# Cross attention's row maxima over two banks at once, and a negation moved to GpSimd

## The chip, the cores and the metric

One core of one Trainium2 chip runs the whole program. The metric is the device time of one execution in microseconds, the median of a few runs. Lower is better. The engines in the text are TensorE (PE in the rows), VectorE (DVE), ScalarE (ACT), GpSimd (POOL) and SyncE (SP); PEld is the loading of TensorE's weights. Matmul results go to PSUM, eight banks of 512 fp32 columns on 128 partitions.

## The reference

A decoder block on x of 8 batches, 256 tokens and 128 features: a self-attention with relative position bias, a cross attention to 1601 context tokens, a second self-attention, a dense layer, and a mixture of 8 experts. Cut to the part that the change touches:

```python
x = x + _L0_attn_ref(_layernorm(x), ...)               # first attention, 16 heads of 8, with a position bias
# in _L0_xattn_ref: input_tensor is layernorm(x), ctx_tensor is ctx_1024 (8, 1601, 128)
q = _split_heads(x @ qw + qb)                          # 16 heads of 8
k = _split_heads(ctx @ kw + kb)
v = _split_heads(ctx @ vw + vb)
scores = jnp.einsum('bqhd,bkhd->bhqk', q, k) / np.sqrt(D // H) + mask
probs = jax.nn.softmax(scores, axis=-1)                # over 1601 keys: needs each row's maximum
out = jnp.einsum('bhqk,bkhd->bqhd', probs, v)
```

## The kernel before

The program runs in phases: the first attention ("A"), the cross attention, the second attention ("S"), a dense tail and the experts. The change touches "A" and the cross attention.

**A unit** of the cross attention is one batch and one pair of heads: 8 batches times 8 pairs p are 64 units. Queries and keys are split in bf16 parts and stacked on 54 rows, one head of the pair on partitions 0 to 53 and the other on 64 to 117 (`half`). The scores are made twice. The first time, queries on the partitions, only for the row maxima: 16 products a unit (2 heads, 2 query tiles `qt`, 4 chunks of 401 or 398 keys), which the program calls grains. Each is a matmul at L1220 into one of the four banks of `GRAIN`, read by one `tensor_reduce` of VectorE at L1436 into a column of `MG`. After the 16th, `negate` (L1443) joins the four chunks' maxima and negates them into `MN`; GpSimd splits `MN` in three bf16 parts (`split_maxima`); TensorE turns them (`max_rows`, L1269), ScalarE copies them into rows of the queries (`place_maxima`, L1364), and so the second product, keys on the partitions, comes out with the maximum subtracted. That second product is 13 score tiles a unit (`scores`, `last_tile`, L1238), two matmuls each, into a ring of three banks that other things share; ScalarE takes the exponential of each (L1356). The `values` matmuls (L1258) then sum the exponentials with the values, in three bursts: tiles 0 to 3, 4 to 7, 8 to 12. A copy by ScalarE (L1372) takes the unit's sums and ends it.

**The order** is written by hand. Every engine walks `cross_plan(p)` once a step and runs the entries that are its own; an entry (what, i, ahead) works on the unit `ahead` of the step's. The plan has 13 places j. At place j stands score tile j + 3 (from place 10 on tiles 0, 1, 2 of the next unit, which I write 0', 1', 2'); at places 3, 7 and 12 a burst of values behind it, and at place 7 the transposes of the next unit's maxima ahead of the burst. The grains are of the unit two ahead: 16 spread over the places, at the end of each place's list. At places 5 and 10 of p = 0 to 5 stands a round of preparation of the next batch's context: p 0 and 1 transposes (T), p 2 and 3 key projection (K), p 4 and 5 value projection (V). Units 6 and 7 of a batch have none, nor has the last batch; I call them quiet. At p = 0 stand also the sums of the batch before ("c"), which VectorE divides.

**The waits** around the maxima: grain n waits until VectorE has read grain n - 4 (`m_read`), so that VectorE has up to four banks ahead of it. TensorE runs in order: a grain that waits holds up the score tiles and bursts behind it. A score tile waits until ScalarE has read the ring's bank three turns before.

**The first attention** has 32 units of four heads. VectorE adds the bias and takes the maxima (L988) into `MG`, then negates the unit's 8 numbers (L1001) into `MN`, and GpSimd splits them (from L1028 on).

## Time and profile before

| | us |
|---|---|
| median of 3 runs | 1321.23 |
| lowest and highest run | 1316.71, 1325.92 |
| span of the profiled execution | 1324.9 |
| cross attention's units, first to last join | 256.3 to 880.8 |

The page gives no time of the profiled execution beside its span, which lies inside the runs' range and 3.7 us over their median. All durations in the text are read from that execution. A row of the timeline merges instructions of one kind; its length is from the first one's start to the last one's end, so that x7 in 3.46 us says how closely they follow each other. The bracket at a row's end is the idle time ahead of it and who ended it.

### The profile page before, as it was taken

The page shows a single profiled execution, that of the slowest core. Times are in us where ns is not written, and L with a number is a line of the kernel's source. Part 1 is how long each engine was busy: PE and PEld are TensorE (multiplying, and loading weights), DVE is VectorE, ACT ScalarE, POOL GpSimd, SP SyncE. Part 2 cuts the span into 40 slices and gives each one's busy share as a digit, 9 for nine tenths or more (in the row PEclk, how much of TensorE's full clock was granted, in tenths as well). Part 3 has the DMA queues.
Part 4 walks back from the last instruction along what each step waited for, and adds up shares of the span by engine and source line. Part 5 has one row for each costly group of instructions (what it writes and reads, how often), then busy time and mean ns, then how long its engine had stood idle before and what let it go on. Part 6 is the DMA issues. An engine that isn't in the chain of part 4 may idle for free. (4 is left out here: it accounts for less than half of the span.)

```text
span 1324.9 us, 33276 instructions
## 1 busy us (share of the span) xinstructions
PE 1104.3 (83%) x12028; PEld 602.7 (45%) x12028; DVE 1018.2 (77%) x2779; ACT 869.6 (66%) x1764; POOL 403.8 (30%) x832
## 2 busy tenths in 40 slices
PE   5799995699999999999999999986688878178894
PEld 2344443244444444444444444433344436167773
DVE  7488857588889898898988889956699968755554
ACT  3488873187887878788788787882488744233443
POOL 3211113223050320405023040021624227545552
PEclk9699997699999999999999999997799989588997
DMA  6970005513232132311323113002740022111113
GB/s 164 213 144 30 2 2 138 133 56 84 67 82 68 39 93 84 72 57 34 101 78 81 49 30 85 21 2 58 149 87 2 2 96 72 56 29 39 39 37 111
DMA packets 76648, 92.31 MB, mean 70 GB/s; under 512 B 8463, under 2 KB 62711, under 8 KB 76488
## 3 DMA queue, kind: packets, MB, share of 16 engines
q1 hardware_dynamic: 72392, 83.90, 25.1%
q0 software_dynamic: 2496, 5.12, 1.5%
q8 instruction: 98, 1.61, 0.5%
q10 hardware_dynamic: 1600, 1.18, 0.3%
q14 instruction: 62, 0.51, 0.1%
HBM read 64.37 MB, written 27.02 MB: 69 GB/s over the span
## 5 line engine op out<-in xcount | busy, mean ns | idle before, releaser
L1436 DVE TENSOR_REDUCE MG<-bank 128x1 f32<-128x401 f32 (+1 forms) x1024 | 515.4, 566 | 75.3 <-PE bank L1220 73.6
L1356 ACT ACTIVATE PT<-bank 128x512 f32<-128x512 f32 (+1 forms) x624 | 334.6, 597 | 64.3 <-PE bank L1238 63.8
L1238 PE MATMUL bank<-QP,KP 54*128 54x256 bf16 (+1 forms) x1664 | 252.4, 274 | 16.3 <-DVE CAT L1451 4.1
L1220 PE MATMUL bank<-KP,QP 54*128 54x401 bf16 (+1 forms) x1024 | 237.0, 344 | 14.8 <-DMA KP<-ctx_k_parts 9.6
L1258 PE MATMUL bank<-PT,VP 128*9 128x256 f32 (+1 forms) x2688 | 197.3, 367 | 0.8 <-ACT XT L1356 0.8
L1511 POOL TENSOR_TENSOR MP<-MN,ZERO 128x4 bf16<-128x4 f32 x128 | 26.4, 206 | 440.8 <-DVE MN L1443 435.8
L1238 PEld LDWEIGHTS bank<-QP,KP 54*128 54x128 bf16 (+1 forms) x1664 | 110.4, 96 | 108.3 <-ACT PT L1356 24.4
L1220 PEld LDWEIGHTS bank<-KP,QP 54*128 54x128 bf16 x1024 | 75.5, 94 | 125.0 <-DVE MG L1436 94.4
L1356 ACT ACTIVATE XT<-bank 128x512 f32<-128x512 f32 (+1 forms) x208 | 116.2, 599 | 20.3 <-PE bank L1238 19.9
L896 PE MATMUL bank<-QP,KP 51*128 51x256 bf16 x512 | 95.7, 281 | 33.6 <-ACT QP L827 8.8
L1258 PEld LDWEIGHTS bank<-PT,VP 128*9 128x9 f32 (+1 forms) x2688 | 76.0, 90 | 57.6 <-issue 20.4
L863 PE MATMUL bank<-KP,QP 51*128 51x256 bf16 x512 | 97.8, 287 | 4.3 <-DVE MN L994 1.4
L988 DVE CUSTOM_DVE_ANT_0 JUNK<-bank,UQ 128x256 bf16<-128x256 f32 x256 | 92.1, 420 | 6.8 <-PE bank L863 6.6
L951 ACT ACTIVATE XT<-bank 128x512 f32<-128x512 f32 x128 | 74.1, 604 | 32.6 <-PE bank L896 32.0
L1258 PE MATMUL bank<-XT,VP 128*9 128x256 f32 (+1 forms) x896 | 91.2, 367 | 0.0
L994 DVE TENSOR_REDUCE MN<-bank 128x2 f32<-128x512 f32 x128 | 81.8, 685 | 4.2 <-POOL MP L1045 1.2
L1028 POOL TENSOR_TENSOR MP<-MN,ZERO 128x8 bf16<-128x8 f32 x128 | 26.4, 206 | 187.8 <-DVE MN L1001 112.4
L896 PEld LDWEIGHTS bank<-QP,KP 51*128 51x128 bf16 x512 | 33.2, 95 | 103.4 <-issue 43.4
L2041 PE MATMUL bank<-WUP,XP 128*128 x234 | 67.8, 427 | 14.6 <-DVE XP L2210 13.5
L827 ACT COPY QP<-bank 3x512 bf16<-3x512 bf16 x96 | 54.8, 571 | 32.4 <-PE bank L932 32.0
L1364 ACT COPY QP<-bank 3x256 bf16<-3x256 bf16 x128 | 45.3, 354 | 26.5 <-DMA q_parts<-PT 25.7
L2218 DVE TENSOR_TENSOR AC<-SI,bank 128x512 f32<-128x512 f32 x39 | 26.8, 688 | 45.5 <-issue 20.7
(281 smaller groups left out, 2007.5 us busy)
## 6 DMA issues: line engine op xcount, KB each, us to landing
KP<-ctx_k_parts SPq DMA_DIRECT2D x128, 100.1 KB
ctx_k_parts<-KPARTS SPq DMA_DIRECT2D x16, 600.4 KB
KP<-ctx_k_parts SPq DMA_DIRECT2D x128, 59.4 KB
CN<-in_ctx SPq DMA_DIRECT2D x8, 768.0 KB
RAW<-in_w_gate_up SPq DMA_DIRECT2D x8, 512.0 KB, 3.8
QP<-q_parts SPq DMA_DIRECT2D x20, 192.0 KB
ctx_k_parts<-KPARTS SPq DMA_DIRECT2D x16, 200.1 KB
UQ<-bias_table SPq DMA_DIRECT2D x4, 768.0 KB, 8.5
```

The costliest lines, as they stand in the source:

```text
L827: last = copy(k.QP[rows, p:p + 2, b * S:(b + 1) * S], PM[:, :].bitcast(BF16)[rows, 0:2 * S].rearrange("r (j n) -> r j n", j=2))
L863: last = nc.tensor.matmul(bank[:, S * qt:S * (qt + 1)], k.QP[rows, p, a:a + 128], k.KP[rows, p, b * S:(b + 1) * S], start=True, stop=True)
L896: last = nc.tensor.matmul(bank[:, S * t:S * (t + 1)], k.KP[half(s), p, a:a + 128], k.QP[half(s), p, b * S:(b + 1) * S], start=not bias, st ...
L951: nc.scalar.activation(PT[n % 8], SCORE[n % 3][:, :], ACT.Exp).then_inc(exp_done, 1)
L988: last = nc.vector.tensor_tensor_reduce(out=JUNK[:, 2 * (n % 2) + q, :], in0=bank[:, S * q:S * (q + 1)], in1=k.UQ[:, 2 * p + s, 128 * q:12 ...
L994: nc.vector.tensor_reduce(MN[:, u % 3, j, s, :], bank[:, :].rearrange("p (q n) -> p q n", q=QT), AX.X, ALU.max, negate=True).then_inc(grai ...
L1220: nc.tensor.matmul(GRAIN[n % NG][:, 0:w], k.QP[half, p, b * S + 128 * qt:b * S + 128 * (qt + 1)], k.KP[half, p, a:a + w], start=True, stop ...
L1238: return nc.tensor.matmul(bank[0:rows[t], S * at:S * (at + 1)], k.KP[half, p, 128 * t:128 * t + rows[t]], k.QP[half, p, b * S:(b + 1) * S] ...
L1258: last = nc.tensor.matmul(k.PO[32 * c:32 * c + HD + 1, q:q + w], VP[b % 2][0:rows[t], t, 2 * p + s, :], PT[(T * g + n) % NP][0:rows[t], S ...
L1356: nc.scalar.activation(PT[n % NP][0:rows[t], :], bank_of("s", g, t)[0:rows[t], :], ACT.Exp).then_inc(exp_done, 1)
L1436: nc.vector.tensor_reduce(MG[:, g % 4, 2 * s + qt, chunk:chunk + 1], GRAIN[n % NG][:, 0:w], AX.X, ALU.max).then_inc(m_read, 1)
L2041: last = nc.tensor.matmul(bank[j % 2], XP[:, j % 2, a, :], WUP[:, bass.ds(e, 1), b, n0:n0 + FF].rearrange("p a n -> p (a n)"), start=(n == ...
```

## The change

In the cross attention the four grain banks become one tensor of four banks, of which `DOUBLE` is banks 0 and 1, or 2 and 3. A grain is now a double: the products of both heads for one query tile and one chunk, into two neighbouring banks, and one `tensor_reduce` of VectorE reads both (128 x 2 x 401) and writes two maxima. A unit has 8 of them. A double waits until the double two before it has been read. `cross_plan` puts the doubles at places 0, 2, 3, 5, 6, 8, 10 and 11, and the join and the split, which stood at the end of a step, behind the first double of the next step (its `ahead` goes from 2 to 1 with that, so it is the same unit's). In the first attention the negation leaves VectorE: GpSimd takes 0 minus the maxima ahead of its split, and waits for that.

```diff
-    k.BANK = [k.stack.enter_context(nc.psum_tensor(f"bank{i}", [128, 512], F32)) for i in range(8)]
+    k.FOUR = k.stack.enter_context(nc.psum_tensor("bank", [128, 4, 512], F32))
+    more = [k.stack.enter_context(nc.psum_tensor(f"bank{i}", [128, 512], F32)) for i in range(4, 8)]
+    k.BANK = [k.FOUR[:, i, :] for i in range(4)] + [bank[:, :] for bank in more]
...
-            def negate(u, i):
-                v.wait_ge(grain_read, 4 * u + 4)
-                if u >= 3:
-                    v.wait_ge(max_split, 4 * (u - 2))
-                nc.vector.tensor_scalar(MN[:, u % 3, :, :, :], MG[:, u % 3, :, :, :], -1.0, None,
-                                        ALU.mult).then_inc(neg_ready, 1)
...
             def split_maxima(u, i):
-                if bias:
-                    pl.wait_ge(neg_ready, u + 1)
-                else:
-                    pl.wait_ge(grain_read, 4 * u + 4)
+                pl.wait_ge(grain_read, 4 * u + 4)
                 if u >= 3:
                     pl.wait_ge(m_turned, u - 2)
+                if bias:
+                    flat = MG[:, u % 3, :, :, :].rearrange("p j s q -> p (j s q)")
+                    nc.gpsimd.tensor_tensor(MN[:, u % 3, :, :, :].rearrange("p j s q -> p (j s q)"),
+                                            ZERO[:, :].broadcast_to(list(flat.shape)), flat,
+                                            ALU.subtract).then_inc(neg_ready, 1)
+                    pl.wait_ge(neg_ready, u + 1)
...
+    doubles = {0: 0, 2: 1, 3: 2, 5: 3, 6: 4, 8: 5, 10: 6, 11: 7}
...
-        plan += [("g", g, 2) for g in range(G * (j + 1) // T if j else 0, min(G, G * (j + 2) // T))]
-    return plan + [("o", 0, 0), ("neg", 0, 2), ("split", 0, 2)]
+        if j in doubles:
+            plan.append(("g", doubles[j], 2))
+        if j == 0:
+            plan += [("neg", 0, 1), ("split", 0, 1)]
+    return plan + [("o", 0, 0)]
...
-                if n >= NG:
-                    pe.wait_ge(m_read, n - NG + 1)
+                if n >= 2:
+                    pe.wait_ge(m_read, n - 1)
...
-                nc.tensor.matmul(GRAIN[n % NG][:, 0:w], k.QP[half, p, b * S + 128 * qt:b * S + 128 * (qt + 1)],
-                                 k.KP[half, p, a:a + w], start=True, stop=True).then_inc(m_ready, 1)
+                for s in (first, 1 - first):
+                    half = slice(HALF * s, HALF * s + CROSS_ROWS)
+                    last = nc.tensor.matmul(DOUBLE[n % 2][:, s, 0:w],
+                                            k.QP[half, p, b * S + 128 * qt:b * S + 128 * (qt + 1)],
+                                            k.KP[half, p, a:a + w], start=True, stop=True)
+                last.then_inc(m_ready, 1)
...
-                nc.vector.tensor_reduce(MG[:, g % 4, 2 * s + qt, chunk:chunk + 1], GRAIN[n % NG][:, 0:w],
+                nc.vector.tensor_reduce(MG[:, g % 4, :, qt, chunk], DOUBLE[n % 2][:, :, 0:w],
                                         AX.X, ALU.max).then_inc(m_read, 1)
```

How the order moves is shown for three places of a quiet unit. The first is TensorE's, from the first burst of values to the transposes of the maxima. Here L1220 are grains, L1238 (L1240 in the changed kernel) score tiles and L1269 (L1271) the transposes; the burst stands right ahead of the first row. Before:

```order
3083 L1220 MATMUL bank<-KP,QP 128x401 x2
3084 L1238 MATMUL bank<-QP,KP 128x256 x2
3085 L1220 MATMUL bank<-KP,QP 128x398
3086 L1238 MATMUL bank<-QP,KP 128x256 x2
3087 L1220 MATMUL bank<-KP,QP 128x398
3088 L1238 MATMUL bank<-QP,KP 128x256 x2
3089 L1220 MATMUL bank<-KP,QP 128x401
3090 L1238 MATMUL bank<-QP,KP 128x256 x2
3091 L1269 MATMUL bank<-IDB,MP 3x128 x4
```

and in the changed kernel the same stretch of TensorE:

```order
2671 L1220 MATMUL bank<-KP,QP 128x401 x2
2672 L1240 MATMUL bank<-QP,KP 128x256 x4
2673 L1220 MATMUL bank<-KP,QP 128x398 x2
2674 L1240 MATMUL bank<-QP,KP 128x256 x2
2675 L1220 MATMUL bank<-KP,QP 128x401 x2
2676 L1240 MATMUL bank<-QP,KP 128x256 x2
2677 L1271 MATMUL bank<-IDB,MP 3x128 x4
```

The three single grains have become two doubles, the second of them (the unit's fifth, d4) ahead of the last score tile.

The second place is TensorE's, from the end of the second burst to the third burst, which follows the last row. Before:

```order
3096 L1220 MATMUL bank<-KP,QP 128x401 x2
3097 L1238 MATMUL bank<-QP,KP 128x256 x2
3098 L1238 MATMUL bank<-QP,KP 65x256
3099 L1220 MATMUL bank<-KP,QP 128x401
3100 L1238 MATMUL bank<-QP,KP 65x256
3101 L1220 MATMUL bank<-KP,QP 128x398
3102 L1238 MATMUL bank<-QP,KP 128x256 x2
3103 L1220 MATMUL bank<-KP,QP 128x401
3104 L1238 MATMUL bank<-QP,KP 128x256 x2
3105 L1220 MATMUL bank<-KP,QP 128x401
3106 L1220 MATMUL bank<-KP,QP 128x398
3107 L1238 MATMUL bank<-QP,KP 128x256 x2
```

and in the changed kernel, same engine, same stretch:

```order
2682 L1240 MATMUL bank<-QP,KP 128x256 x2
2683 L1240 MATMUL bank<-QP,KP 65x256
2684 L1220 MATMUL bank<-KP,QP 128x401 x2
2685 L1240 MATMUL bank<-QP,KP 65x256
2686 L1240 MATMUL bank<-QP,KP 128x256 x2
2687 L1220 MATMUL bank<-KP,QP 128x401 x2
2688 L1240 MATMUL bank<-QP,KP 128x256 x2
2689 L1220 MATMUL bank<-KP,QP 128x398 x2
2690 L1240 MATMUL bank<-QP,KP 128x256 x2
```

Two grains stood between the burst and score tile 11; now tile 11 comes first and the double d5 behind it. Two grains or one double (d7) stand ahead of the last row, tile 2'.

The third place is VectorE's, the first two units of the cross attention (L1436 and L1438 are the reduces, L1443 and L1445 the join). Before:

```order
767 L1436 TENSOR_REDUCE MG<-bank 128x1 x16
768 L1443 TENSOR_REDUCE MN<-MG 128x4
769 L1436 TENSOR_REDUCE MG<-bank 128x1 x16
770 L1443 TENSOR_REDUCE MN<-MG 128x4
```

and in the changed kernel:

```order
735 L1438 TENSOR_REDUCE MG<-bank 128x2 x9
736 L1445 TENSOR_REDUCE MN<-MG 128x4
737 L1438 TENSOR_REDUCE MG<-bank 128x2 x8
738 L1445 TENSOR_REDUCE MN<-MG 128x4
```

The join of a unit has moved behind the next unit's first reduce, and half as many reduces stand between two joins.

## Rows read from the trace of the kernel before

**Rows 1.** The page: the span, and busy time of each engine.

```profile
span 1324.9 us, 33276 instructions
...
PE 1104.3 (83%) x12028; PEld 602.7 (45%) x12028; DVE 1018.2 (77%) x2779; ACT 869.6 (66%) x1764; POOL 403.8 (30%) x832
```

**Rows 2.** Eight cross units by windows: stretch, its length, busy us (instructions), clock, DMA.

```profile
410.00:490.00 80.00, 75.15 (x897) 36.18 (x895) 70.27 (x152) 64.88 (x137) 20.60 (x48) 1.00 0.24 65
```

**Rows 3.** The page, costliest groups: two reduces of VectorE that read PSUM.

```profile
L1436 DVE TENSOR_REDUCE MG<-bank 128x1 f32<-128x401 f32 (+1 forms) x1024 | 515.4, 566 | 75.3 <-PE bank L1220 73.6
...
L994 DVE TENSOR_REDUCE MN<-bank 128x2 f32<-128x512 f32 x128 | 81.8, 685 | 4.2 <-POOL MP L1045 1.2
```

**Rows 4.** Line L1443, the join of a unit's maxima: ns min/median/max, first and last start.

```profile
L1443 DVE TENSOR_REDUCE MN<-MG x64: 169/170/171, 256.3 to 880.8; 128x4 f32<-128x16 f32 x64
```

**Rows 5.** Timeline, ScalarE: the copies that end units 60, 61 and 62.

```profile
871.79 0.37 ACT L1372 COPY OT<-bank 128x256 f32<-128x256 f32 x1 [0.52 <-PE bank L1258]
...
880.58 0.37 ACT L1372 COPY OT<-bank 128x256 f32<-128x256 f32 x1 [0.51 <-PE bank L1258]
...
888.77 0.37 ACT L1372 COPY OT<-bank 128x256 f32<-128x256 f32 x1 [0.27 <-PE bank L1258]
```

**Rows 6.** Timeline, TensorE, one quiet unit: start, length, line, tile, count.

```profile
646.18 0.28 PE L1238 MATMUL bank<-QP,KP 54*128 54x256 bf16 x1
...
648.56 0.34 PE L1220 MATMUL bank<-KP,QP 54*128 54x401 bf16 x2
...
650.38 0.23 PE L1269 MATMUL bank<-IDB,MP 128*3 128x128 bf16 x2 [0.19 <-ACT XT L1356]
...
651.46 0.34 PE L1220 MATMUL bank<-KP,QP 54*128 54x401 bf16 x2
...
651.64 0.38 PE L1238 MATMUL bank<-QP,KP 54*128 54x256 bf16 x3
...
652.95 0.82 PE L1220 MATMUL bank<-KP,QP 54*128 54x401 bf16 x2
...
653.44 0.39 PE L1238 MATMUL bank<-QP,KP 54*128 54x256 bf16 x2
...
654.96 0.28 PE L1238 MATMUL bank<-QP,KP 54*128 54x256 bf16 x1
```

**Rows 7.** Timeline, VectorE, the same unit.

```profile
648.93 2.50 DVE L1436 TENSOR_REDUCE MG<-bank 128x1 f32<-128x401 f32 x5 [0.21 <-PE bank L1220]
...
651.84 3.46 DVE L1436 TENSOR_REDUCE MG<-bank 128x1 f32<-128x401 f32 x7 [0.41 <-PE bank L1220]
...
655.33 0.17 DVE L1443 TENSOR_REDUCE MN<-MG 128x4 f32<-128x16 f32 x1
```

**Rows 8.** Timeline, ScalarE, the same unit.

```profile
652.06 2.52 ACT L1356 ACTIVATE PT<-bank 128x512 f32<-128x512 f32 x5 [0.26 <-PE bank L1238]
```

**Rows 9.** Timeline, all engines, a unit with two rounds of key projection.

```profile
605.53 0.37 ACT L1372 COPY OT<-bank 128x256 f32<-128x256 f32 x1 [0.63 <-PE bank L1258]
...
611.24 0.34 PE L1220 MATMUL bank<-KP,QP 54*128 54x401 bf16 x2
...
611.83 0.60 ACT L1356 ACTIVATE PT<-bank 128x512 f32<-128x512 f32 x1 [0.23 <-PE bank L1238]
...
612.48 0.94 PE L1291 MATMUL bank<-CT,WQK 128*128 128x401 f32 x2
...
615.52 0.37 ACT L1372 COPY OT<-bank 128x256 f32<-128x256 f32 x1 [0.49 <-PE bank L1258]
```

**Rows 10.** Timeline of the first attention: VectorE's idle time, GpSimd's last split, TensorE's next transposes.

```profile
143.35 0.06 DVE L986 MEMSET TOUCH<- 1x1 f32 x1 [0.91 <-PE bank L863]
...
143.38 0.21 POOL L1045 TENSOR_TENSOR MP<-MN,MP 128x8 bf16<-128x8 f32 x1
...
145.08 0.33 PE L932 MATMUL bank<-IDB,MP 128*3 128x128 bf16 x5
```

**Rows 11.** Timeline, VectorE, the first cross unit's maxima.

```profile
248.44 7.79 DVE L1436 TENSOR_REDUCE MG<-bank 128x1 f32<-128x401 f32 x16 [9.28 <-PE bank L1220]
```

More of the change, by code:

```diff
@@ L136, in allocate @@
     k.HALF = k.sb("HALF", [128, NT])
-    k.BANK = [k.stack.enter_context(nc.psum_tensor(f"bank{i}", [128, 512], F32)) for i in range(8)]
-    k.RING = [bank[:, :] for bank in k.BANK]
+    k.FOUR = k.stack.enter_context(nc.psum_tensor("bank", [128, 4, 512], F32))
+    more = [k.stack.enter_context(nc.psum_tensor(f"bank{i}", [128, 512], F32)) for i in range(4, 8)]
+    k.BANK = [k.FOUR[:, i, :] for i in range(4)] + [bank[:, :] for bank in more]
+    k.RING = list(k.BANK)
     k.PO, k.PX = k.BANK[6], k.BANK[7]
@@ L1014, in _ @@
             actions = {"g": maxima, "c": divide}
-            if bias:
-                actions["neg"] = negate
-            else:
+            if not bias:
                 actions["m"] = lambda u, i: copy_maxima(nc.vector.tensor_copy, v, u, (1,), m_rows_second)
@@ L1080, in cross_plan @@
             plan.append(("v", bursts[j], 0))
-        plan += [("g", g, 2) for g in range(G * (j + 1) // T if j else 0, min(G, G * (j + 2) // T))]
-    return plan + [("o", 0, 0), ("neg", 0, 2), ("split", 0, 2)]
+        if j in doubles:
[3 more added lines that the diff above has]
+    return plan + [("o", 0, 0)]
 def grain_order(chunks):
-    rest = [[(s, qt, u, a, w) for qt in range(QT) for u, (a, w) in enumerate(chunks)] for s in range(2)]
+    places = [(qt, u, a, w) for qt in range(QT) for u, (a, w) in enumerate(chunks)]
     order, half = [], 0
-    for what, i, _ in cross_plan(PAIRS - 1):
+    for what, d, _ in cross_plan(PAIRS - 1):
         if what == "s":
-            half = 1 - i % 2 if i < NTILES - 1 else 0
+            half = 1 - d % 2 if d < NTILES - 1 else 0
         if what == "g":
-            order.append((rest[half] or rest[1 - half]).pop(0))
-            half = 1 - half
+            order.append((half, *places[d]))
     return order
@@ L1124, in phase_cross @@
     nc = k.nc
-    T, N, G = NTILES, NCTX, 16
+    T, N, G = NTILES, NCTX, 8
     rows = [min(128, N - 128 * t) for t in range(T)]
@@ L1134, in phase_cross @@
     GRAIN, RING = k.BANK[0:4], [k.BANK[4], k.BANK[5], k.PX]
-    NG = len(GRAIN)
+    DOUBLE = [k.FOUR[:, 0:2, :], k.FOUR[:, 2:4, :]]
     TURNS = cross_ring()
@@ L1151, in phase_cross @@
         OT = k.sb("OT", [128, NO, S], stack=st)
-        MG = k.sb("MG", [128, 4, 4, 4], stack=st)
+        MG = k.sb("MG", [128, 4, 2, QT, 4], stack=st)
         MN = k.sb("MN", [128, 4, 4], stack=st)
@@ L1204, in take_bank, with grain @@
                 return RING[n % 3]
-            def grain(g, u):
-                n = G * g + u
+            def grain(g, d):
+                n = G * g + d
                 b, p = batch_of(g)
-                s, qt, _, a, w = grains[u]
-                half = slice(HALF * s, HALF * s + CROSS_ROWS)
-                if n >= NG:
-                    pe.wait_ge(m_read, n - NG + 1)
+                first, qt, _, a, w = grains[d]
+                if n >= 2:
+                    pe.wait_ge(m_read, n - 1)
                 if n == 0:
@@ L1215, in grain @@
                     pe.wait_ge(q_taken, 4)
-                if p == 0 and u == 0 and b % 2 == 0:
+                if p == 0 and d == 0 and b % 2 == 0:
                     pe.wait_ge(qk_in[b // 2], Q_LOADS)
-                if u == 0:
+                if d == 0:
                     pe.wait_ge(kp_in[p], LOADS * (b + 1))
-                nc.tensor.matmul(GRAIN[n % NG][:, 0:w], k.QP[half, p, b * S + 128 * qt:b * S + 128 * (qt + 1)],
-                                 k.KP[half, p, a:a + w], start=True, stop=True).then_inc(m_ready, 1)
+                for s in (first, 1 - first):
[4 more added lines that the diff above has]
+                last.then_inc(m_ready, 1)
             def scores(g, i):
@@ L1428, in _, with maxima @@
             nc.vector.memset(k.PO[:, :], 0.0).then_inc(psum_cleared, 1)
-            def maxima(g, u):
-                n = G * g + u
-                s, qt, chunk, a, w = grains[u]
-                if u == 0 and g >= 4:
+            def maxima(g, d):
+                n = G * g + d
+                _, qt, chunk, a, w = grains[d]
+                if d == 0 and g >= 4:
                     v.wait_ge(neg_ready, g - 3)
                 v.wait_ge(m_ready, n + 1)
-                nc.vector.tensor_reduce(MG[:, g % 4, 2 * s + qt, chunk:chunk + 1], GRAIN[n % NG][:, 0:w],
+                nc.vector.tensor_reduce(MG[:, g % 4, :, qt, chunk], DOUBLE[n % 2][:, :, 0:w],
                                         AX.X, ALU.max).then_inc(m_read, 1)
@@ L1514, in split_maxima @@
                 pl.wait_ge(neg_ready, g + 1)
+                x, parts = MN[:, g % 4, :], [MP[:, g % 4, :, a] for a in range(3)]
                 if g >= 4:
                     pl.wait_ge(m_turned, g - 3)
-                x, parts = MN[:, g % 4, :], [MP[:, g % 4, :, a] for a in range(3)]
                 copy(parts[0], x).then_inc(max_split, 1)
```

10 lines of the change are left out of this document (4 added, 6 removed).

## The prediction

> **What bounds the kernel now.** I went from the page to the stretch, then to one unit. The page says that TensorE is busy 83% and VectorE 77% of the span [rows 1], a mean over phases. In the cross attention a stretch of 80 us, eight units, has TensorE 75.15, VectorE 70.27 and ScalarE 64.88 us busy at the full granted clock [rows 2]: three engines that are all nearly full, so the pace is set by how they wait for each other. The single reduce takes 515.4 us of VectorE in all [rows 3], and a reader could stop there and call VectorE the bound. Joins come every (880.8 - 256.3) / 63 = 9.91 us [rows 4].
>
> The rows that decide are the ends of three units. Unit 61 takes 880.58 - 871.79 = 8.79 us, and unit 62, the first in which no grains are left, 888.77 - 880.58 = 8.19 us [rows 5]. Taking away all grains and all the reduces gives 0.60 us a unit; so that is the most a cheaper maximum can give in a quiet unit. VectorE isn't the bound; TensorE and ScalarE pass the work to each other, and the grains add a little to that chain.
>
> Where, one quiet unit shows. I count from its first score tile at 646.18 [rows 6]. The first burst ends at 2.38, where two grains start; the transposes of the maxima start at 4.20 and wait for an exponential; the second burst ends at 5.28, where two grains start ahead of score tile 11 at 5.46; ScalarE has idled for that tile and starts at 5.88 [rows 8]; two grains start at 6.77 and, by the length of the merged row (0.82 us, one lasts 0.34), at 7.25; tile 2' follows at 7.26; the next unit starts at 8.78. So the grains lie on the chain in three places: 0.18 us behind the first burst, 0.18 us behind the second, and the last grain's wait, 0.2 to 0.3 us, which holds tile 2' and the third burst. They sum to the 0.60. The last is a true wait for VectorE: it started on the grains of 5.28 at 651.84 after 0.41 us idle, takes one each (3.46 - 0.566) / 6 = 0.482 us [rows 7], and so has read the third at 7.19.
>
> **The double reduce.** Single: 566 ns for 401 columns. The reduce of 512 columns into two results takes 685 ns [rows 3]: (685 - 566) / 111 = 1.07 ns a column, and nothing for the second result. A double has 802 columns: 566 + 401 x 1.07 = 0.995, and I take 0.985, with 1.04 ns a column, which fits 566 with a fixed part of 0.148. No row reads across two banks, so the bounds are 0.95 and, with the fixed part paid twice, two singles at 1.13. I take the low row-based value, since the 685 ns row is the nearest. Back to back, two singles cost 2 x 0.482 = 0.965 and a double some 0.90: that frees 0.065 x 8 = 0.5 us of VectorE a unit, and the join behind another reduce some 0.07 more. It was not the bound, so none of it counts as such. Only what the double does to the three places counts.
>
> The timeline's single reduces overlap: they follow each other in 0.482 us and last 0.566. The Trainium skill's page Advanced Engine Details and Errata (The Read-Write Bubble) says that PSUM's latency is exposed between instructions, and advises large operands. By that rule a merged pair would save the whole fixed 0.148 us, 512 x 0.148 = 76 us of VectorE; by the rows 0.065, 33 us. And rows 5 say that neither may be taken off the kernel's time.
>
> **Quiet unit, walked through.** Behind the first burst (2.38) stands double d2, whose two matmuls run on different halves of the rows: two grains of different heads last 0.34 us together, as one does [rows 6]. VectorE starts 0.37 us behind the issue (648.56 to 648.93 [rows 6, 7]), at 2.75, and ends at 3.74. Nothing gained here: tile 7 still waits the 0.18. New: d4 stands ahead of tile 10 and waits for d2's read, till 3.80 (release takes 0.06: the read that started at 652.32 ends at 652.89, the grain starts at 652.95). Tile 10 then goes at 3.97 to 4.18, where it went before 3.85; the transposes wait for ScalarE until 4.20 anyway. Slack left: 0.02 us. The second burst ends at 5.28 as before, but tile 11 now starts at 5.28 instead of 5.46: its exponential, and all behind it, is 0.18 earlier. d5 follows at 5.50; VectorE reads it from 5.88 to 6.86; d7 waits for that until 6.92, takes 0.17 as both halves are its own, and tile 2' starts at 7.10, not 7.26. From tile 2' to the next unit is 8.78 - 7.26 = 1.52, so the unit takes 8.62. Gain 0.16 us. The exponential of tile 12 (5.70 + 0.48 + 0.60, the steps from rows 8) would have allowed 6.8, so d5's read is the chain: the double still costs some 0.25 us there. Quiet units with grains: p 6 and 7 of seven batches and p 1 to 5 of the last, 19. 19 x 0.16 = 3.0 us.
>
> **Units with preparation.** The K unit of 605.53 to 615.52 takes 9.99 us [rows 9]. Its second key projection (612.48) waits for the exponential of tile 11 (611.83 + 0.60), and that tile stands behind two grains at 611.24. With tile 11 ahead of d5 I gain 0.18, or a little more, as ScalarE had idled 0.23 for it. The projection's 0.87 us then cover d5's read, so d7 waits for nothing, and of the two grains ahead of the third burst at most their issue stays: 0.25 us a unit, bounds 0.18 and 0.35. T and V units have the same order with other rounds; a V round's first part is held by VectorE's additions, which start when the projection ends, so there it is the second half that gains too. 35 units x 0.25 = 8.8 us. The eight units p = 0 are held at first by VectorE's division, which the change doesn't touch, then by the same second half: 8 x 0.25 = 2.0 us.
>
> **Start.** The first unit's maxima run alone: 16 in 7.79 us [rows 11]. Eight doubles take 0.985 + 7 x 0.90 = 7.3. Two units run so: 1.0 us.
>
> **Moved join and split.** The join comes at about 1.5 us of the unit instead of at its start, and GpSimd's split follows with four steps of some 0.21 us [rows 10] and the waits between them, 1.2 us; the transposes come at 4.20. Slack above 1 us; in K units GpSimd is late from its own key splits by more than that, before as after. Zero; with no cover it would cost up to 1.3 us a unit.
>
> **First attention.** VectorE loses a negation of 0.17 us and had 0.91 us idle behind it. GpSimd gains an operation, some 0.25 us with its wait; its split ended at 143.59, and TensorE turns maxima next at 145.08 [rows 10], and those of an earlier unit at that. Zero, bounds -1 and +2 us over the phase.
>
> **Sum.** 3.0 + 8.8 + 2.0 + 1.0 = 14.8 us, off the profiled 1324.9 as well as off the median of 1321.2: 1306.4.
>
> **Rivals.**
> 1. *VectorE's freed time counts* (chance 0.17). If d5's read holds nothing, for instance as its matmuls slip in sooner, quiet units gain up to 0.42 and the others 0.45: 62 x 0.44 = 27 us, 1294. For it: the 0.60 of rows 5. Against: it needs 0.25 us less in each chain than my walk finds.
> 2. *Little is left* (0.25). The walk has 0.02 us slack at the transposes. A double read of 1.08 us gives back 0.1 at the transposes and again at d7, and a T or V unit may be held by a bank of the ring that I took as free. Gain 3 to 9 us: 1315.
> 3. *Two doubles are coarser than four singles* (0.13). TensorE, in order, stands at d4 and d7 with score tiles and a burst behind, until a whole double has been read. From a read of about 1.13 us on the quiet unit loses. At 1.3 us (a price for crossing banks, or both banks being written next door), d4 goes at 4.11, the transposes at 4.50, d5 at 5.8, d7 at 7.55, tile 2' at 7.72, 0.46 late: 62 x 0.46 = +28, 1350; at 1.2 us some +10, 1331.
> A rule speaks for rival 3: the page Perfetto Trace Analysis (Optimizing Tensor Performance, Matmuls) of the Trainium skill wants independent groups to rotate through different banks, so that reading one overlaps the next one's matmuls. The change keeps four banks but rotates by two. The 0.41 us idle of VectorE in rows 7 is what such a rule would see grow.
> 4. *The change doesn't do what it says* (in with 2): a negation or a join that sits on a path; the order's rows show it where the diff puts it, so at most 0.02.
>
> **Numbers.** My forecast, 1306, has 0.45, its own range 1298 to 1314, most of it (0.28) over 1% faster. 1%, 13 us, is about what a measurement of this kernel can tell, as the three runs lie 9 us apart. Faster by over 1%: 0.28 + 0.17, and a little of 2: 0.47. Slower by over 1%: 0.11. Within: 0.42. The range from 1290 to 1326 takes in rivals 1 and 2, and the edge of 3.
>
> **What would show it.** In the changed profile: the double at 980 to 1000 ns (1130 favours rival 3); quiet units at 8.62 apart, K units at 9.75; ScalarE's idle time ahead of tile 11's exponential down from 0.26 to 0.1 or less; the last reduce ahead of d7 ending right before it; tile 10 directly ahead of the transposes without idle time; VectorE's idle ahead of the reduce at 5.88 some 0.4 us, as it has less to do. The first attention unchanged in length. It is wrong if the double's read or its issue to start (0.37) is longer, if the two matmuls of a double don't run together, or if an exponential's bank, not d5, holds the second half.

## The result, and the profile after

The changed kernel takes 1305.88 us (median of 4 runs, 1303.31 to 1307.97) against 1320.88: a ratio of 0.9885, 95% interval 0.9854 to 0.9916. The forecast was 1306.4. That the sum comes so near is in part luck: two of its terms are too large, one is too small by more than these, and a wait that it didn't have takes some back.

The page of the changed kernel, its span, its busy times and the group of the double's reduce:

```profile
span 1304.4 us, 32735 instructions
...
PE 1070.0 (82%) x12028; PEld 590.0 (45%) x12028; DVE 976.7 (75%) x2235; ACT 868.9 (67%) x1764; POOL 413.7 (32%) x864
...
L1438 DVE TENSOR_REDUCE MG<-bank 128x2 f32<-128x802 f32 (+1 forms) x512 | 488.1, 988 | 91.0 <-PE bank L1220 83.7
```

Against [rows 1, 3]: VectorE has 41.5 us less to do, TensorE 34 us, and the span is 20.5 us shorter. The same stretch as [rows 2] by windows, and the join's line, answering to [rows 4]:

```profile
410.00:490.00 80.00, 74.56 (x925) 36.42 (x923) 68.09 (x91) 66.50 (x140) 21.50 (x52) 1.00 0.25 67
```

```profile
L1445 DVE TENSOR_REDUCE MN<-MG x64: 158/159/169, 254.8 to 864.2; 128x4 f32<-128x16 f32 x64
```

Joins now come every (864.2 - 254.8) / 63 = 9.67 us, before 9.91. ScalarE, whose work per unit is unchanged, does more of it in 80 us: 66.50 against 64.88.

All comparisons below use two figures that every trace gives. **The cross time** goes from the first to the last of the 64 copies that end a unit: 620.29 us before, 605.93 after, 14.36 less. **The unit times** are the distances between those copies, and repeat within 0.01 us from batch to batch, but for the last batch, the waits for keys in units p = 6 (named near the end) and single units in which TensorE's granted clock falls. Of the profile's 20.5 us only these 14.4 and 1.9 ahead of them lie in phases that the change touches; the rest, 4.2 us, lies behind the cross attention in phases with the same code. From the last copy to the end the twelve kernels of this text take between 421.8 and 429.7 us, in no order that follows the edits.

**The clock.** A unit of the kernel before and one of the changed kernel, both p = 0, have a granted clock of 0.87 where all other units from the first to the last copy have 1.00. By windows, as in [rows 2]: that unit of the kernel before, an ordinary p = 0 unit of it, and that unit of the changed kernel:

```profile
743.89:757.47 13.58, 12.64 (x145) 5.77 (x143) 10.69 (x21) 8.95 (x19) 0.81 (x4) 0.87 0.15 47
663.88:676.05 12.17, 11.17 (x145) 5.33 (x143) 10.55 (x21) 8.82 (x18) 0.82 (x4) 1.00 0.24 68
```

```profile
807.64:820.62 12.98, 11.20 (x137) 4.90 (x135) 9.63 (x11) 7.93 (x16) 0.82 (x4) 0.87 0.16 51
```

Within the unit the clock is at its lower level, 0.50 (1.2 of 2.4 GHz), for some 3.4 us. In the kernel before TensorE had been busy for 1.33 of the 2.00 us up to 750 and for 0.73 of the next one; its other p = 0 units have the same waits at the same places and keep the clock. The fall costs 1.41 us in the kernel before (13.58 against 12.17). The changed kernel's lies in the last batch, 12.98 against 11.2 to 11.5 in e3, e7, e9 and e10, so some 1.5. Both kernels have one, and so they nearly cancel in the difference of 14.4. e1, e2, e4, e5 and e8 have one too, and e1 and e8 a second in their last unit, of 1.05 us; e3, e6, e7, e9 and e10 have none. So the cross times of these last five stand some 1.5 us too low beside the others, and nothing shows that their order is the reason: e1 has TensorE's program of the kernel before, and its clock falls in another batch, and a second time.

One quiet unit of the changed kernel, TensorE's timeline, answering to [rows 6]:

```profile
565.38 0.28 PE L1240 MATMUL bank<-QP,KP 54*128 54x256 bf16 x1
...
567.76 0.34 PE L1220 MATMUL bank<-KP,QP 54*128 54x401 bf16 x2
...
569.20 0.34 PE L1220 MATMUL bank<-KP,QP 54*128 54x401 bf16 x2 [0.49 <-DVE MG L1438]
569.38 0.38 PE L1240 MATMUL bank<-QP,KP 54*128 54x256 bf16 x2
569.69 0.23 PE L1271 MATMUL bank<-IDB,MP 128*3 128x128 bf16 x2
569.71 0.40 PE L1260 MATMUL bank<-PT,VP 128*9 128x256 f32 x2
...
570.77 0.39 PE L1240 MATMUL bank<-QP,KP 54*128 54x256 bf16 x3
570.91 0.42 PE L1220 MATMUL bank<-KP,QP 54*128 54x401 bf16 x2
...
572.42 0.34 PE L1220 MATMUL bank<-KP,QP 54*128 54x398 bf16 x2 [0.18 <-DVE MG L1438]
572.60 0.38 PE L1240 MATMUL bank<-QP,KP 54*128 54x256 bf16 x2
...
574.11 0.28 PE L1240 MATMUL bank<-QP,KP 54*128 54x256 bf16 x1
```

and VectorE's, answering to [rows 7], with the reduces of d5, d6 and d7 in the last row:

```profile
566.96 0.16 DVE L1445 TENSOR_REDUCE MN<-MG 128x4 f32<-128x16 f32 x1
567.04 3.90 DVE L1438 TENSOR_REDUCE MG<-bank 128x2 f32<-128x802 f32 x4
571.37 2.79 DVE L1438 TENSOR_REDUCE MG<-bank 128x2 f32<-128x802 f32 x3 [0.43 <-PE bank L1220]
```

and ScalarE's, answering to [rows 5, 8]:

```profile
565.52 0.37 ACT L1374 COPY OT<-bank 128x256 f32<-128x256 f32 x1 [0.52 <-PE bank L1260]
...
571.20 1.08 ACT L1358 ACTIVATE XT<-bank 128x512 f32<-128x512 f32 x2 [0.18 <-PE bank L1240]
...
574.25 0.37 ACT L1374 COPY OT<-bank 128x256 f32<-128x256 f32 x1 [0.52 <-PE bank L1260]
```

From 565.38: d2 at 2.38; d4 at 3.82, having waited 0.49 us for d2's read; tile 10 at 4.00; the transposes at 4.31; tile 11 at 5.39, d5 at 5.53, its read at 5.99; d7 at 7.04, again right behind the read that it waits for (571.37 + 0.99, and 0.06); tile 2' at 7.22; the next unit at 8.73. The walk had 3.80, 3.97, **4.20**, 5.28, 5.50, 5.88, 6.92, 7.10 and 8.62. Up to tile 10 it is 0.03 us late at most. One step doesn't hold, from tile 10 to the transposes: 0.31 us, where the walk had 0.21. The transposes come 0.11 us late, and that stays to the end. One sign of the prediction's list isn't there either: ScalarE still idles 0.18 us ahead of tile 11's exponential, where 0.1 or less was expected.

The K unit that answers to [rows 9], timeline of all engines:

```profile
595.34 0.37 ACT L1374 COPY OT<-bank 128x256 f32<-128x256 f32 x1 [0.63 <-PE bank L1260]
...
600.97 0.39 PE L1240 MATMUL bank<-QP,KP 54*128 54x256 bf16 x3
...
601.40 0.60 ACT L1358 ACTIVATE PT<-bank 128x512 f32<-128x512 f32 x1
...
602.05 0.94 PE L1293 MATMUL bank<-CT,WQK 128*128 128x401 f32 x2
...
603.58 1.05 PE L1260 MATMUL bank<-PT,VP 128*9 128x256 f32 x16
...
604.92 0.37 ACT L1374 COPY OT<-bank 128x256 f32<-128x256 f32 x1 [0.32 <-PE bank L1260]
```

From copy to projection 6.71 us, before 6.95: 0.24 gained. ScalarE no longer idles for tile 11's exponential. From there to the unit's end 2.87, before 3.04: another 0.17, which the forecast didn't have. The third burst shows it, 1.53 us behind the projection; before, it came 1.71 behind (614.19 - 612.48), timeline of TensorE in the kernel before:

```profile
614.19 0.62 PE L1258 MATMUL bank<-PT,VP 128*9 128x256 f32 x8
```

Between the projection and this burst the kernel before has three grains (at 613.36, and two from 613.75 on), the changed one four, the two doubles d6 and d7: one matmul more in 0.17 us less. TensorE, before and then in the changed kernel:

```profile
613.36 0.34 PE L1220 MATMUL bank<-KP,QP 54*128 54x401 bf16 x1
613.54 0.40 PE L1238 MATMUL bank<-QP,KP 54*128 54x256 bf16 x4
613.75 0.50 PE L1220 MATMUL bank<-KP,QP 54*128 54x401 bf16 x2
```

```profile
602.92 0.34 PE L1220 MATMUL bank<-KP,QP 54*128 54x401 bf16 x2
```

### The profile page after: what moved, and what is told of

It reads as the page before. It is cut to its first block and busy times, and to the rows that moved or that the text cites. A ratio compares the mean times of both kernels' runs of the same rounds, so it can differ in the third digit from the quotient of the medians.

```text
span 1304.4 us, 32735 instructions
## 1 busy us (share of the span) xinstructions
PE 1070.0 (82%) x12028; PEld 590.0 (45%) x12028; DVE 976.7 (75%) x2235; ACT 868.9 (67%) x1764; POOL 413.7 (32%) x864
## 5 line engine op out<-in xcount | busy, mean ns | idle before, releaser
L1438 DVE TENSOR_REDUCE MG<-bank 128x2 f32<-128x802 f32 (+1 forms) x512 | 488.1, 988 | 91.0 <-PE bank L1220 83.7
L1240 PE MATMUL bank<-QP,KP 54*128 54x256 bf16 (+1 forms) x1664 | 241.5, 275 | 14.7 <-DVE CAT L1453 4.1
L1220 PE MATMUL bank<-KP,QP 54*128 54x401 bf16 (+1 forms) x1024 | 205.6, 343 | 34.0 <-DVE MG L1438 21.5
L1240 PEld LDWEIGHTS bank<-QP,KP 54*128 54x128 bf16 (+1 forms) x1664 | 100.5, 95 | 124.5 <-ACT PT L1358 42.7
L1220 PEld LDWEIGHTS bank<-KP,QP 54*128 54x128 bf16 x1024 | 69.6, 95 | 111.2 <-DVE MG L1438 58.9
L2102 ACT ACTIVATE SI<-bank 128x512 f32<-128x512 f32 x39 | 23.4, 599 | 52.1 <-PE bank L2043 47.4
```

The source lines that it names most:

```text
L1220: last = nc.tensor.matmul(DOUBLE[n % 2][:, s, 0:w], k.QP[half, p, b * S + 128 * qt:b * S + 128 * (qt + 1)], k.KP[half, p, a:a + w], start= ...
L1240: return nc.tensor.matmul(bank[0:rows[t], S * at:S * (at + 1)], k.KP[half, p, 128 * t:128 * t + rows[t]], k.QP[half, p, b * S:(b + 1) * S] ...
L1438: nc.vector.tensor_reduce(MG[:, g % 4, :, qt, chunk], DOUBLE[n % 2][:, :, 0:w], AX.X, ALU.max).then_inc(m_read, 1)
```

## The experiments

All kernels in one table: median of 2 (e6) to 10 runs, ratio to the kernel before of the same chip with its 95% interval, unit times for p = 1 (T), 2 and 3 (K), 4 and 5 (V), 6 and 7 (quiet) and 0, and the cross time. The units of p = 0 are those with the clock at 1.00, the quiet ones those without a wait for keys.

| kernel | us | ratio | T | K | V, p 4 | V, p 5 | quiet | p 0 | cross |
|---|---|---|---|---|---|---|---|---|---|
| before | 1320.88 | | 9.49 | 9.99 | 10.72 | 10.08 | 8.78 | 12.18 | 620.3 |
| changed | 1305.88 | 0.9885 (0.9854-0.9916) | 9.33 | 9.58 | 10.21 | 9.81 | 8.72 | 11.77 | 605.9 |
| e1 | 1322.60 | 1.0000 (0.9980-1.0020) | 9.50 | 9.99 | 10.72 | 10.08 | 8.78 | 12.18 | 621.4 |
| e2 | 1309.94 | 0.9902 (0.9870-0.9933) | 9.33 | 9.58 | 10.21 | 9.94 | 8.85 | 11.89 | 609.9 |
| e3 | 1313.73 | 0.9930 (0.9907-0.9953) | 9.49 | 9.75 | 10.38 | 9.98 | 8.63 | 11.94 | 609.1 |
| e4 | 1309.77 | 0.9899 (0.9867-0.9930) | 9.33 | 9.58 | 10.21 | 9.81 | 8.72 | 11.76 | 606.0 |
| e5 | 1319.02 | 0.9968 (0.9945-0.9990) | 9.39 | 9.82 | 10.54 | 9.98 | 8.91 | 12.00 | 617.2 |
| e6 | 1294.58 | 0.9794 (0.9767-0.9821) | 9.33 | 9.58 | 10.21 | 9.74 | 8.36 | 11.61 | 594.8 |
| e7 | 1323.50 | 1.0009 (0.9993-1.0026) | 9.72 | 9.88 | 10.61 | 10.37 | 8.76 | 12.17 | 619.5 |
| e8 | 1334.67 | 1.0114 (1.0057-1.0172) | 9.50 | 10.13 | 10.72 | 10.00 | 9.09 | 12.35 | 630.5 |
| e9 | 1302.75 | 0.9856 (0.9833-0.9879) | 9.33 | 9.48 | 10.21 | 9.98 | 8.63 | 11.78 | 601.9 |
| e10 | 1301.56 | 0.9855 (0.9829-0.9881) | 9.33 | 9.58 | 10.21 | 9.81 | 8.62 | 11.61 | 601.8 |

**e1, the negation alone.** The kernel before, with only the first attention's negation moved:

```diff
-                nc.vector.tensor_scalar(MN[:, u % 3, :, :, :], MG[:, u % 3, :, :, :], -1.0, None,
-                                        ALU.mult).then_inc(neg_ready, 1)
+                    nc.gpsimd.tensor_tensor(MN[:, u % 3, :, :, :].rearrange("p j s q -> p (j s q)"),
+                                            ZERO[:, :].broadcast_to(list(flat.shape)), flat,
+                                            ALU.subtract).then_inc(neg_ready, 1)
```

> The kernel before with the first attention's negation moved to GpSimd, and nothing else of the change. Theory (the negation was hidden on VectorE and is hidden on GpSimd): no change, within 1 us of 1321, and the first attention's units stay 4.0 us apart. Rival (the profile of the changed kernel starts its first cross reduce 1.7 us earlier, at 246.7 instead of 248.4, so the negation paid): 1319.5, and the first cross reduce at 246.7.

The ratio is 1.000. VectorE's busy time falls from 1018.2 to 1011.6 us and nothing follows: the first attention's units stay 4.03 us apart. The 1.1 us more of cross time lie in the last unit alone (8.57 us against 7.51), where the clock falls. The first cross reduce starts at 245.9, even earlier than the rival had it, but so it does in e5 (245.0), which leaves the negation on VectorE: its start tells nothing of the edit. So the negation is worth zero within 0.2%.

**e2, the doubles' order with single reduces.** All of the change, but VectorE reads the two banks of a double with an instruction each:

```diff
-                nc.vector.tensor_reduce(MG[:, g % 4, :, qt, chunk], DOUBLE[n % 2][:, :, 0:w],
-                                        AX.X, ALU.max).then_inc(m_read, 1)
+                for s in range(2):
+                    last = nc.vector.tensor_reduce(MG[:, g % 4, s, qt, chunk:chunk + 1], DOUBLE[n % 2][:, s, 0:w],
+                                                   AX.X, ALU.max)
+                last.then_inc(m_read, 1)
```

> The changed kernel, but VectorE reads each double with two single reduces of 401 columns; order and waits of TensorE stay those of the change. Theory (the order on TensorE gives the gain, not the merged instruction): units with key projection stay at 9.6 us, quiet units go from 8.72 to 8.80 as the second read ends 0.08 us later, and the time is 1308 to 1310. Rival (VectorE's saved time gives the gain): units with key projection return to 9.9, quiet ones to 8.8, the time to 1318 or more.

10.4 of the 14.4 us of cross time are there without the merged instruction. T, K and the first V unit are exactly those of the changed kernel: where a preparation holds the unit, the merged read is worth nothing. It is worth 0.13 us in quiet and second V units and 0.12 at p = 0, 4.0 us in all; for the quiet unit 0.08 was expected.

**e3, d5 ahead of tile 11.** In the changed kernel one double goes a place earlier:

```diff
-    doubles = {0: 0, 2: 1, 3: 2, 5: 3, 6: 4, 8: 5, 10: 6, 11: 7}
+    doubles = {0: 0, 2: 1, 3: 2, 5: 3, 6: 4, 7: 5, 10: 6, 11: 7}
```

> The changed kernel with one entry moved back: the sixth double (d5) at place 7, right behind the second burst and ahead of score tile 11, where the two single grains had stood. Theory: units with key projection lose 0.17 (9.58 to 9.75), as their second projection waits for tile 11's exponential; quiet units gain up to 0.1 (8.72 to 8.62), as their chain runs through d5's read. Together +5 us, 1311. Rival (VectorE's time counts): nothing changes, 1306.

The K unit goes to 9.75, 0.17 longer: this is what tile 11's place is worth there. The quiet unit goes to 8.63, 0.09 shorter: there d5's read, not tile 11, holds the second half. Both were expected, and so was the sum: 3.2 us more cross time than the changed kernel, 4.7 without the clock.

**e4, the join back at the step's end**, with the doubles as changed:

```diff
-        if j == 0:
-            plan += [("neg", 0, 1), ("split", 0, 1)]
-    return plan + [("o", 0, 0)]
+    return plan + [("o", 0, 0), ("neg", 0, 2), ("split", 0, 2)]
```

> The changed kernel with join and split back at the end of the step (behind the unit's last double, ahead 2). Theory: VectorE is idle 0.6 us ahead of the next unit's first reduce, so a join there costs nothing on the chain: quiet units 8.72, key projection units 9.58, the time within 1 us of the changed kernel's. Rival (the later join is what saves, as a wait for the last read's end goes): 0.07 to 0.1 us a unit, +4 to +6 us.

Every unit time is that of the changed kernel, and so is the cross time to 0.1 us. The median lies 3.9 us over it, where less than 1 was expected; the profile has 5.3 us more behind the cross attention, in code that is the same, and the intervals of the two ratios overlap. The later join costs and brings nothing.

**e5, tile 11 ahead of two single grains**, in the kernel before:

```diff
-        plan += [("g", g, 2) for g in range(G * (j + 1) // T if j else 0, min(G, G * (j + 2) // T))]
+        if j != 7:
+            plan += [("g", g, 2) for g in range(9 if j == 8 else G * (j + 1) // T if j else 0, min(G, G * (j + 2) // T))]
```

> The kernel before with one move: the two single grains behind the second burst stand behind score tile 11 instead of ahead of it. Single reduces, four single banks, join at the end. Theory (order): units with key projection gain 0.2 (9.99 to 9.79), quiet units nothing or lose 0.05 (8.78 to 8.83), together -7 us, 1314. Rival (the gain is in the doubles): no change, 1321.

K gains 0.17, the first V unit 0.18, and the quiet unit loses 0.13: singles that start later are read later. In all 3.1 us of cross time, of 7 expected. So tile 11's place gives a K unit 0.17, by e3 as by e5, and the other 0.24 of its 0.41 comes with the doubles. The stretches of a K unit say the same: back ahead of tile 11 (e3), d5 moves the second projection from 6.71 to 6.88 us and leaves the 2.87 behind it as they are; e5 brings it from 6.95 to 6.78 and leaves the 3.04. Tile 11's place acts ahead of the projection alone.

**e6, nearly free reads.** Each reduce reads 8 of a bank's 401 (or 398) columns, so the maxima are of those only; the matmuls are all there:

```diff
-                nc.vector.tensor_reduce(MG[:, g % 4, :, qt, chunk], DOUBLE[n % 2][:, :, 0:w],
+                nc.vector.tensor_reduce(MG[:, g % 4, :, qt, chunk], DOUBLE[n % 2][:, :, 0:8],
```

> The changed kernel whose reduces of doubles read 8 columns of each bank instead of 401, so that the maxima are those of 8 keys in each chunk (the rest of their reading is left out); everything else stays. It shows all that VectorE's reading still costs. Theory (only the two waits of a quiet unit are VectorE's): quiet units 8.38 instead of 8.72, units with key or value projection within 0.1 of 9.58 and 10.21, together -8 to -11 us in the cross attention. Rival (VectorE still sets the pace): every unit gains 0.5 us or more, -30 us.

The page of this kernel, busy times and the reduce:

```profile
PE 1072.0 (83%) x12028; PEld 592.7 (46%) x12028; DVE 582.7 (45%) x2235; ACT 866.6 (67%) x1764; POOL 410.7 (32%) x864
...
L1438 DVE TENSOR_REDUCE MG<-bank 128x2 f32<-128x16 f32 x512 | 87.2, 175 | 443.4 <-PE bank L1220 441.0
```

VectorE falls from 75% to 45% of the span, 394 us less work, and the cross time falls by 11.1 us, some 1.5 of which are the clock: 0.36 us a quiet unit, 0.16 at p = 0, 0.07 in the second V unit, nothing in T, K and the first V units. This measures what the double's read still costs, and shows that VectorE isn't the bound.

**e7, every double behind a tile or ahead of a burst**, to give back the 0.1 us at the transposes: d2 behind tile 7, d4 between the transposes and the burst, d7 between tile 2' and the burst.

```diff
-    doubles = {0: 0, 2: 1, 3: 2, 5: 3, 6: 4, 8: 5, 10: 6, 11: 7}
+    doubles = {0: 0, 2: 1, 4: 2, 5: 3, 7: 4, 8: 5, 10: 6, 12: 7}
...
             if bursts[j] == 1:
                 plan.append(("m", 0, 1))
+            if j in (7, 12):
+                plan.append(("g", doubles[j], 2))
             plan.append(("v", bursts[j], 0))
-        if j in doubles:
+        if j in doubles and j not in (7, 12):
```

> The changed kernel with the score tile ahead of the double at three more places: d2 behind tile 7, d4 behind tile 10 and the transposes of the maxima (ahead of the burst), d7 behind tile 2' (ahead of the burst). Theory: quiet units 8.46 to 8.5 instead of 8.72, as tile 7 goes 0.18 earlier and the transposes no longer stand behind d4's wait; units with key projection stay at 9.58; the time -4 to -6 us, 1301. Rival (a double issued later is read later and holds the next one): quiet units 8.7 to 8.9, no gain.

A miss: no faster than the kernel before. TensorE's timeline of a quiet unit, transposes (L1273), d4, burst (L1262) and tile 11:

```profile
647.67 0.28 PE L1273 MATMUL bank<-IDB,MP 128*3 128x128 bf16 x4 [0.19 <-ACT XT L1360]
647.88 0.34 PE L1222 MATMUL bank<-KP,QP 54*128 54x401 bf16 x2
648.16 1.05 PE L1262 MATMUL bank<-PT,VP 128*9 128x256 f32 x16
649.14 0.39 PE L1242 MATMUL bank<-QP,KP 54*128 54x256 bf16 x3
```

From transposes to tile 11 it takes 1.47 us; in the changed kernel 570.77 - 569.69 = 1.08, with the burst's first row at 569.71, only 0.02 behind the transposes. A double costs 0.17 to 0.18 of its own. The other 0.2 us are, as I read the rows, what the transposes cost once the double keeps them from running together with the burst; e9 tests that.

**e8, a double of one head.** The same 8 doubles, reads and places, but a double holds two chunks of one head, so that its two matmuls use the same half of the rows:

```diff
-                for s in (first, 1 - first):
+                for c in range(2):
+                    a, w = chunks[u + c]
                     half = slice(HALF * s, HALF * s + CROSS_ROWS)
-                    last = nc.tensor.matmul(DOUBLE[n % 2][:, s, 0:w],
+                    last = nc.tensor.matmul(DOUBLE[n % 2][:, c, 0:w],
...
-                nc.vector.tensor_reduce(MG[:, g % 4, :, qt, chunk], DOUBLE[n % 2][:, :, 0:w],
+                nc.vector.tensor_reduce(MG[:, g % 4, s, qt, u:u + 2], DOUBLE[n % 2][:, :, 0:w],
```

> The changed kernel with a double made of two chunks of one head instead of one chunk of both heads, so that its two matmuls use the same half of TensorE's rows; the last 3 of 1601 keys' neighbours (3 columns of the third chunk) are left out of the maxima. Same number of reduces, same places. Theory (the two heads of a double run side by side, and that packing gave the 0.17 us behind the second projection that I had not counted): units with key projection lose 0.15 to 0.35 (9.58 to 9.75 or 9.9), the cross attention 8 to 16 us. Rival (packing is nothing, TensorE has room): 0.

24.6 us of cross time over the changed kernel, 1.05 of them the clock in the last unit: more than expected, and slower than the kernel before. A K unit takes 0.55 us more, a quiet one 0.37. The K unit's first projection starts at 2.91 us, as in the kernel before (changed: 2.74), and from its second one to its end it takes 3.22 us instead of 2.87, twice 0.17 for the two doubles there. The timeline of TensorE has the pair in 0.51 us, where the changed kernel has it in 0.34:

```profile
664.20 0.51 PE L1221 MATMUL bank<-KP,QP 54*128 54x401 bf16 x2 [0.31 <-DVE MG L1440]
```

**e9 and e10, what e7 should have been.** The transposes stay beside the burst, and d4 stands behind tile 10 and ahead of them. e9 has also d2 behind tile 7 and d7 behind tile 2'. e10 moves d4 alone:

```diff
-    doubles = {0: 0, 2: 1, 3: 2, 5: 3, 6: 4, 8: 5, 10: 6, 11: 7}
+    doubles = {0: 0, 2: 1, 3: 2, 5: 3, 7: 4, 8: 5, 10: 6, 11: 7}
...
             if bursts[j] == 1:
+                plan.append(("g", doubles[j], 2))
                 plan.append(("m", 0, 1))
...
-        if j in doubles:
+        if j in doubles and j not in (7, 12):
```

> The changed kernel with d2 behind score tile 7, d4 behind tile 10 but ahead of the transposes (so that the transposes still run side by side with the burst behind them), and d7 behind tile 2' ahead of the third burst. Theory (what the run with d4 between transposes and burst lost was that overlap: 1.47 us from the transposes to tile 11 there, 1.08 in the changed kernel): that stretch is 1.08 again, quiet units take 8.45 to 8.55, units with key projection 9.5 to 9.58, the cross attention 601 to 603 us from first to last sum, the time 1301. Rival (a double read later holds the next one): quiet units 8.7 or more, the time 1308 or more.

> The changed kernel with one entry moved: d4 behind score tile 10, still ahead of the transposes. Theory: the transposes no longer stand behind tile 10's issue behind d4's wait, quiet units 8.62 instead of 8.72, units with key projection 9.58 or 0.1 less, the time -2 to -4 us, which only the units show. Rival: no change in any unit.

Both reach 602 us of cross time. e9 differs from e7 in one thing, d4 ahead of the transposes and not behind them, and that is worth 17.7 us of cross time: 0.39 to 0.40 us in every unit but the quiet ones, the 1.47 - 1.08 of the timelines, and 0.13 in those. Its quiet unit takes 8.63 us, not the 8.45 to 8.55 expected, so d2 and d7 behind their tiles bring nothing there. Against e10, e9 gains 0.10 more in K units and gives 0.17 back in the second V unit and at p = 0. They are measured at 0.9856 and 0.9855 of the kernel before, and their cross times lie 4.1 us below the changed kernel's. Some 1.5 of that are the clock, so the order is worth about 2.6 us. The intervals of the ratios overlap with the changed kernel's; it is the unit times that tell them apart. e10 is the simpler version of the two. TensorE's timeline of a quiet unit of e10, first tile, d2, tile 10, d4, transposes, tile 11, d7, tile 2' and the next unit:

```profile
642.34 0.28 PE L1241 MATMUL bank<-QP,KP 54*128 54x256 bf16 x1
...
644.72 0.34 PE L1221 MATMUL bank<-KP,QP 54*128 54x401 bf16 x2
...
645.97 0.39 PE L1241 MATMUL bank<-QP,KP 54*128 54x256 bf16 x2 [0.30 <-ACT PT L1359]
646.16 0.37 PE L1221 MATMUL bank<-KP,QP 54*128 54x401 bf16 x2
646.55 0.23 PE L1272 MATMUL bank<-IDB,MP 128*3 128x128 bf16 x2
...
647.62 0.39 PE L1241 MATMUL bank<-QP,KP 54*128 54x256 bf16 x3
...
649.27 0.34 PE L1221 MATMUL bank<-KP,QP 54*128 54x398 bf16 x2 [0.18 <-DVE MG L1439]
649.45 0.38 PE L1241 MATMUL bank<-QP,KP 54*128 54x256 bf16 x2
...
650.96 0.28 PE L1241 MATMUL bank<-QP,KP 54*128 54x256 bf16 x1
```

Tile 10 no longer waits behind d4 (3.63 instead of 4.00), the transposes come at 4.21 and the unit ends at 8.62. From the transposes on these are the times that the prediction's walk gave the changed kernel, reached by another order.

## Why the prediction came out, term by term

**The sum.** Of the forecast's 14.8, 13.8 lie in the cross time, which fell by 14.36, made up like this.

| term | forecast | measured |
|---|---|---|
| quiet, 19 units | 0.16 each, 3.0 | 0.06 each, 1.1 |
| preparation, 35 units | 0.25 each, 8.8 | 7 x (0.16 + 2 x 0.41 + 0.51 + 0.27) = 12.3 |
| p = 0 | 8 x 0.25 = 2.0 | 2.2, over the 7 between copies (0.40 in each of the first five, the two falls of the clock in the others) |
| key loads | not seen | -1.25 |
| sum | 13.8 | 14.4 |

Two terms of the forecast were too large by 2.7 us together (quiet units 1.9, the start 0.8), the preparation too small by 3.5, and the keys took 1.25 that it didn't have; nothing in the prediction says that these would cancel.

The forecast's start term, 1.0 us for two units, lies ahead of the first copy. First reduce to first copy was 275.99 - 248.44 = 27.55 us, and is 274.04 - 246.73 = 27.31. The maxima of both units lie in that stretch, so 0.24 is all that shows of the 1.0. The first reduce itself started between 244.4 and 248.4 us in all kernels, in no order that follows the edits, so the 1.7 us at which it came earlier is no gain of the change.

**The double reduce** was sized right: 988 ns with 985 forecast, and no price for crossing from one bank to the next. How nine of them follow each other, VectorE at the start, answering to [rows 11]:

```profile
246.73 8.18 DVE L1438 TENSOR_REDUCE MG<-bank 128x2 f32<-128x802 f32 x9 [10.42 <-PE bank L1220]
```

(8.18 - 0.99) / 8 = 0.90 us each, as forecast. e2 and the changed kernel differ by 1005.9 - 976.7 = 29 us of VectorE's busy time, against 33 by the rows. The Trainium skill's page Advanced Engine Details and Errata (The Read-Write Bubble) has PSUM's latency exposed between instructions; by that, merging would have saved 76 us. The traces side with the rows: single reduces already overlapped. The other rule, on rotating groups through different banks (the Trainium skill's page Perfetto Trace Analysis, Optimizing Tensor Performance, Matmuls), is borne out in one of two places. VectorE's idle time, where the prediction looked for it, didn't grow: 0.43 us ahead of d5's read, and 0.41 before. But TensorE now waits 0.49 us at d4, which the walk had, and with tile 10 behind it this costs the 0.1 us that e10 gives back.

**Quiet units: the mis-sized term.** The step that failed is "Slack left: 0.02 us" at the transposes. It took the step from tile 10 to the transposes from the kernel before as 0.21 us; with tile 10 delayed behind d4 TensorE needs 0.31. This is the mechanism that rival 2 named for its 0.1 us, though not with its cause: the read was not longer. e10 takes it away and the unit is 8.62. Why 0.31 and not 0.21 is not shown: the second of tile 10's two matmuls starts 0.11 us behind the first, and the transposes 0.20 behind that one, with no wait for another engine on record. The rest of the walk, that d5's read holds the second half, is shown by e3 (0.09 shorter when d5 goes earlier) and e6 (0.36 with nearly no read: the 0.1 at the transposes, and 0.26, where the forecast had 0.25 left).

**Units with preparation: too small.** The forecast had tile 11 in it, 0.18 or a little more; its place is worth 0.17 by e3 and e5. The mis-sized part is the rest: 0.07 was left for it in the 0.25, and it measured 0.24, of which 0.07 ahead of the second projection and 0.17 behind it. What the prediction had not priced is that the kernel before leaves some grains without a partner of the other head beside them, and the changed one none. e8 undoes just that, in all doubles, and K units lose 0.55, more than the whole gain of 0.41. e2 and e6 leave the 2.87 us behind the projection as they are, so neither the merged read nor VectorE's time is what gives the 0.17, and e8 prices one unpaired double there at 0.17. How it divides between pairing and the places of d6 and d7 was not measured apart.

**Zero terms.** The negation is zero by e1, the join by e4, and both were forecast so.

**What was not foreseen.** In units p = 6 of three batches TensorE waits for the next batch's keys, and they take 9.26, 9.23 and 8.92 us, not 8.72. The waits of TensorE from 400 to 800 us in the changed kernel (total, times, longest), with the largest ahead of them:

```profile
PE bank L1220 <- DVE MG L1438: 9.5, 32, 0.5
...
PE bank L1220 <- DMA KP<-ctx_k_parts: 1.4, 3, 0.6
```

All units of the kernel before have 8.78 or 8.79 there. It comes back in all kernels but e1 and e7 and is most in e10 (9.11, 9.46 and 8.94), so further gains in the units with preparation may be partly lost to it. A load that starts sooner was not tried.

**The rivals.** Rival 1, that VectorE's freed time counts, needed 0.44 us a unit and is refuted by e6. Rival 3 needed a read of over 1.13 us, and it was 0.99. Rival 2 shows in the quiet units alone. The merged instruction, which gives the change its name, brings 4.0 of the 14.4 us; 10.4 come from what stands where on TensorE, the two heads' matmuls side by side and tile 11 ahead of a double. Tile 11's place alone gave 3.1 in the kernel before (e5). That pairing gives most of the other 7.3 is argued from e8, which takes it from every double at once; no run gave it alone to the kernel before.

## What to carry to other kernels

When three engines are each 80 to 95% busy and hand work to each other, price an edit by walking one period of each kind with its waits, not by the busy time it removes: 394 us off VectorE were worth about 10. A walk is only as good as its smallest slack, so a step with 0.02 us left is a term of the range and not of the sum, and moving the one instruction that uses the slack up is the next edit to try. And ask what an edit does to neighbours that run side by side: two such pairs, the heads' matmuls and the transposes with the burst, cost 23.5 and 17.7 us when taken apart (e8, and e7 against e9), where the merged instruction is worth 4.0. Last, compare unit by unit ahead of comparing sums: one fall of the clock moved a cross time by 1.5 us, over a third of what e10 seemed to gain.

## What the runs showed of the hardware

- Two matmuls of 54 rows on different halves of TensorE's rows take 0.34 us together, on the same half 0.51. Over the cross attention that is some 23.5 us (e8, without its last unit's clock), more than the whole change.
- Transposes with 3 output rows and the burst of values behind them (9 output rows each) start 0.02 us apart and take 1.08 us together; with a double between them 1.47 us, of which its own time explains 0.17 to 0.18 (e7). The same double ahead of the transposes is cheaper by 17.7 us over the cross attention (e9).
- A reduce over two banks costs as much as its columns: 988 ns for 802, 175 ns for 16 and two results: (988 - 175) / 786 = 1.03 ns a column and a fixed part of 0.16 us. At that price the 401 columns of a single reduce (566 ns) leave 0.15 us, so the second bank adds no fixed part of its own.
- The granted clock of TensorE fell to 0.50 for some 3.4 us once or twice in a cross attention in seven of the twelve traces and not in the others, and in different batches with the same program of TensorE (batch 6 in the kernel before, batch 4 and the last unit in e1). A fall in a p = 0 unit cost 1.41 us.
